# A four-layer audio tower: the third layer's experts, all eight against the two that the gate picks

## The chip, the cores and the metric

One core of one Trainium2 chip runs the whole tower in one launch. The metric is the device time of that launch in microseconds (us), the median of several runs. The five engines (TensorE or PE, VectorE or DVE, ScalarE or ACT, GpSimd or POOL, SyncE or SP) each run a program of their own and meet only at semaphores.

## What is computed

Four sequences of 748 tokens (width 128) pass four layers, each an attention and a feed-forward part. The change is in the third layer's feed-forward part, a mixture of eight experts. Its gate works on the whole sequence: tokens are pooled into one vector for each batch, so that one pair of experts is picked for all 748 tokens. The reference computes all eight experts and multiplies six of them by zero:

```python
def _L2_ffn_ref(x, attn_w, attn_b, gate_w, gate_b, w1, b1, w2, b2):
    scores = x @ attn_w + attn_b
    aw = jax.nn.softmax(scores, axis=1)
    pooled = jnp.sum(x * aw, axis=1)
    gates = jax.nn.softmax(pooled @ gate_w + gate_b, axis=-1)
    _, idx = jax.lax.top_k(gates, 2)
    mask = jnp.sum(jax.nn.one_hot(idx, 8, dtype=gates.dtype), axis=-2)
    g = gates * mask
    g = g / (jnp.sum(g, axis=-1, keepdims=True) + 1e-09)
    h = jax.nn.gelu(jnp.einsum('bsd,edh->ebsh', x, w1) + b1[:, None, None, :], approximate=False)
    eo = jax.nn.gelu(jnp.einsum('ebsh,eho->ebso', h, w2) + b2[:, None, None, :], approximate=False)
    return jnp.einsum('ebso,be->bso', eo, g)
```

The hidden width is 512 (four tiles of 128, `FT`). The fourth layer's experts, whose gate picks for each token, are all computed, before and after.

## The kernel before

All is f32 in this part. The kernel has a front (layers one and two's attention), a long middle (layer two's experts), and from about 2975 us a tail with layers three and four. The tail's work is a list, `TAIL`, that every engine walks in the same order, each doing its own share of a step. It is made of four parts for each batch: part 0 is layer three's attention, with the pooling and the gate at its end (steps `pool` and `gate`); part 1 is layer three's experts (steps `up2`, `down2`, then `back2`, which turns their sum back and adds it to `h`) and a norm (`measure`, `normalise`, `turn`); part 2 is layer four's attention; part 3 is layer four's norm, gate and experts. Part 0 and part 1 of batch 0 stand alone. After that part 2 of batch b - 1 is woven with part 0 of batch b, and part 3 of batch b - 1 with part 1 of batch b. The last batch's parts 2 and 3 stand alone again.

`woven` (line 469) merges two parts by the share of their cost that is done: each step has a cost written by hand in `tail_steps` (line 432), and steps are sorted by the middle of their share. So the order depends on the costs and on the number of steps; nothing is moved while it runs. Even batches use lane 0's buffers, odd ones lane 1's (`k` is the lane).

An expert is four `up2` steps (two matmuls each: 128x128 weights against 384 or 364 columns) and two `down2` steps (four matmuls each, summed in PSUM). ScalarE takes each product out with a gelu, into `hid` or into `outs2`, which are two tiles of `masked`. VectorE's `merge2` (line 2607) copies the expert's gate value into a column, multiplies the expert's output by it and adds it to `sum2` (in `KT`), then frees the weights. TensorE's side of this is `second` (line 1560) with `job`, whose matmul is line 1556; it waits for the result of three matmul groups before, four PSUM banks being in use. The weights of an expert are 128 rows of 1029 values, 514.5 KB. SyncE loads them (`load_second`, line 774) into two slots in turn, as soon as `wts_free` says that a slot is free, so that the first two of a batch are there long before the batch's gate.

`gating_parts` (line 2210) is the gate on VectorE, a chain of tiny steps with a drain behind each: maximum, first pick, then, after ScalarE's exponential, second pick and the gate values. It serves three gates: layer two's, layer three's (one row) and layer four's (six tiles).

`fuse` multiplies pairs of layer four's attention weights together, ahead of their use in part 2. It is made in two portions: `EARLY` (four heads) inside the last norm of batch 0's part 0, `LATE` (four heads) inside the norm at the end of batch 0's part 1. After `LATE` TensorE signals `third_free`, upon which SyncE may load the fourth layer's expert weights (2060 KB) over the third layer's.

SyncE's own program, in order: weights of batch 0's experts; fourth layer's weights after `third_free`; then for b = 1 to 3 the next batch's `hn`, the experts' weights of batch b, and the stores of batch b - 1, which wait for its result.

## Time and profile before

| | before |
|---|---|
| median of 3 runs | 4555.29 us (4553.76 to 4556.07) |
| span of the profiled execution | 4551.8 us |
| PE busy | 4137.7 us, 91% |
| ACT busy | 2872.1 us, 63% |
| DVE busy | 2766.0 us, 61% |
| POOL busy | 708.1 us, 16% |
| DMA moved | 160.46 MB, mean 35 GB/s |
| tail (from 2975 us), by share of the chain that ended last from 3060 us on | PE L1556 28.3% |

The profile is of one execution. Its span runs from the first to the last instruction and is 3.5 us below the median of the runs. Busy times of an engine are sums of durations; TensorE's matmuls overlap one another, so their durations add up to more than the time they take, and their distance from start to start is the better price. An f32 matmul shows as two records. PEclk is the share of the full clock that was granted: 1.00 is 2.4 GHz and 0.50 is 1.2 GHz.

### The profile page before, as it was taken

What the parts mean: (1) busy time and instruction counts of PE and PEld (TensorE: products, weight loads), DVE (VectorE), ACT (ScalarE), POOL (GpSimd) and SP (SyncE); (2) the same over time, 40 slices, a digit from 0 to 9 for tenths busy, and PEclk for the clock granted to TensorE, in tenths of its full rate; (3) what the DMA queues carried; (4) which work ended last, traced back from release to release, by engine and by line L of the source; (5) the groups of instructions that cost most, each with busy time, mean ns of one, the idle gap of its engine ahead of it and who ended that gap; (6) DMA issues with size and microseconds to landing.
All of it is one profiled execution on the core that took longest, in us unless ns stands there. A gap on an engine that the chain in (4) does not pass through costs nothing.

```text
span 4551.8 us, 67714 instructions
## 1 busy us (share of the span) xinstructions
PE 4137.7 (91%) x25107; PEld 2324.2 (51%) x25107; DVE 2766.0 (61%) x6426; ACT 2872.1 (63%) x6118; POOL 708.1 (16%) x484
## 2 busy tenths in 40 slices
PE   7787599999999999999999999868889888988988
PEld 5464344444444444444444444435556555655666
DVE  5656477777777777777777777422442444344254
ACT  3232278777877787777878787674664574474533
POOL 1000212232322222222222232100000000000000
PEclk9878699999999999999999999989999999999999
DMA  2000233333424242424243333000000000000000
GB/s 109 7 21 1 43 45 47 46 52 45 60 43 61 37 60 43 60 39 54 43 53 56 48 50 41 24 32 28 32 1 24 22 1 15 27 1 1 29 4 4
DMA packets 94713, 160.46 MB, mean 35 GB/s; under 512 B 18305, under 2 KB 75058, under 8 KB 94130
## 3 DMA queue, kind: packets, MB, share of 16 engines
q1 hardware_dynamic: 94386, 156.14, 20.6%
q8 instruction: 201, 3.29, 0.3%
q14 instruction: 126, 1.03, 0.1%
HBM read 73.97 MB, written 7.82 MB: 18 GB/s over the span
## 4 chain that ended last, share of the span: by engine, by line
PE 74%; DVE 9%; issue 6%; ACT 6%; DVEq 2%; PEld 1%; POOL 1%; PEldq 0%; DMA 0%; POOLq 0%; SPq 0%; ACTq 0%
PE ps L1190 12%; PE ps L1226 12%; PE ps L1200 10%; PE ps L1556 9%; PE ps L1260 4%; PE ps L1269 4%; PE ps L1181 2%; PE ps L1077 2%; PE ps L1688 2%; PE ps L1488 2%; PE ps L1289 2%; PE ps L1626 1%; DVE peaks L2274 1%; PE ps L1650 1%; PE ps L1062 1%
## 5 line engine op out<-in xcount | busy, mean ns | idle before, releaser
L2274 DVE TENSOR_REDUCE peaks<-ps 128x1 f32<-128x748 f32 (+1 forms) x1536 | 1408.8, 933 | 482.4 <-PE ps L1200 459.5
L1845 ACT ACTIVATE masked<-ps 128x384 f32<-128x384 f32 (+3 forms) x1536 | 683.7, 486 | 193.6 <-PE ps L1190 181.1
L1845 ACT ACTIVATE probs<-ps 128x384 f32<-128x384 f32 (+1 forms) x1536 | 662.4, 484 | 73.9 <-PE ps L1190 73.7
L923 POOL TENSOR_TENSOR rstd<-var,minus_half 128x6 f32<-128x6 f32 x104 | 138.4, 1331 | 2823.8 <-DVE var L2500 1495.0
L1190 PE MATMUL ps<-shared 98*128 98x384 bf16 (+3 forms) x1536 | 447.6, 327 | 4.5 <-ACT probs L1845 1.7
L1190 PE MATMUL ps<-q_stack,k_stack 98*128 98x384 bf16 (+3 forms) x1536 | 450.3, 328 | 1.2
L1200 PE MATMUL ps<-k_stack,q_stack 96*128 96x374 bf16 (+1 forms) x1536 | 380.6, 329 | 35.3 <-DMA k_stack<-parts 21.8
L1200 PE MATMUL ps<-shared 96*128 96x374 bf16 (+1 forms) x1536 | 372.1, 323 | 7.4 <-DVE peaks L2274 6.9
L1190 PEld LDWEIGHTS ps<-shared 98*128 98x128 bf16 (+1 forms) x1536 | 148.0, 103 | 337.2 <-ACT masked L1845 126.2
L1190 PEld LDWEIGHTS ps<-q_stack,k_stack 98*128 98x128 bf16 (+1 forms) x1536 | 149.6, 103 | 329.9 <-ACT masked L1845 121.2
L1200 PEld LDWEIGHTS ps<-k_stack,q_stack 96*128 96x128 bf16 (+1 forms) x1536 | 154.8, 105 | 157.6 <-DVE peaks L2274 42.2
L1200 PEld LDWEIGHTS ps<-shared 96*128 96x128 bf16 (+1 forms) x1536 | 155.9, 104 | 115.5 <-issue 38.1
L1260 PE MATMUL ps<-attT,wr 128*128 128x364 f32 (+1 forms) x512 | 208.8, 492 | 2.7
L1973 ACT ACTIVATE hid<-ps,wts 128x384 f32<-128x384 f32 (+1 forms) x256 | 146.3, 573 | 88.9 <-PE ps L1556 77.6
L1269 PE MATMUL ps<-hid,wr 128*128 128x364 f32 (+1 forms) x512 | 171.0, 477 | 0.0
L1556 PE MATMUL ps<-hid,wts 128*128 128x364 f32 (+1 forms) x512 | 169.9, 479 | 0.0
L1886 ACT ACTIVATE hid<-ps,wr 128x384 f32<-128x384 f32 (+1 forms) x256 | 139.9, 572 | 44.4 <-PE ps L1260 41.1
L1226 PE MATMUL ps<-masked,shared 128*32 128x384 f32 (+3 forms) x1536 | 160.5, 490 | 0.6 <-ACT masked L1845 0.6
L1226 PE MATMUL ps<-masked,V 128*32 128x384 f32 (+3 forms) x1536 | 160.5, 490 | 0.0
L1226 PE MATMUL ps<-probs,V 128*32 128x384 f32 (+1 forms) x1536 | 160.5, 490 | 0.0
L1226 PE MATMUL ps<-probs,shared 128*32 128x384 f32 (+1 forms) x1536 | 160.5, 490 | 0.0
L1556 PEld LDWEIGHTS ps<-hid,wts 128*128 128x128 f32 x512 | 96.7, 192 | 60.5 <-issue 2.3
(584 smaller groups left out, 7646.7 us busy)
## 6 DMA issues: line engine op xcount, KB each, us to landing
shared<-parts SPq DMA_DIRECT2D x192, 187.0 KB, 9.1
wr<-in_l SPq DMA_DIRECT2D x32, 580.5 KB, 3.5
q_stack<-parts SPq DMA_DIRECT2D x96, 187.0 KB, 8.0
k_stack<-parts SPq DMA_DIRECT2D x96, 187.0 KB, 10.5
wts<-in_l SPq DMA_DIRECT2D x32, 514.5 KB, 3.6
wrow<-in_l_rows SPq DMA_DIRECT2D x32, 320.0 KB, 4.0
wq<-in_l SPq DMA_DIRECT2D x32, 192.0 KB, 3.4
shared<-in_tv SPq DMA_DIRECT2D x1, 4096.0 KB, 27.1
```

The costliest lines, as they stand in the source:

```text
L923: pool.tensor_tensor(lane.rstd, lane.var, minus_half[:, :], ALU.pow).then_inc(S["rstd_ready"], 1)
L1077: mm = pe.matmul(ps[:, 4 + t % 4, 0:width], lhs, rhs, start=(i == 0), stop=(i == len(terms) - 1))
L1190: pe.matmul(out[0:m, 0:hi - lo], k_stack[k][0:STACK + SHIFT, head, j * P:j * P + m], q_stack[k][0:STACK + SHIFT, head, lo:hi], start=True, ...
L1200: mm = pe.matmul(out[0:m, a, 0:T // 2], q_stack[k][0:STACK, head, j * P:j * P + m], k_stack[k][0:STACK, head, a * T // 2:(a + 1) * T // 2] ...
L1226: mm = pe.matmul(ps[at:at + PLACE, 6, 0:hi - lo], V32[x % 2][0:m, j, head, :], probs_ring(SIDE * b + i)[0:m, 0:hi - lo], start=(j == 0), s ...
L1260: pe.matmul(out[:, 0:hi - lo], wr[:, WR_UP + f * P:WR_UP + (f + 1) * P], attT[:, lo:hi], start=True, stop=True).then_inc(S["ring_ready"], 1)
L1269: mm = pe.matmul(out[:, 0:hi - lo], wr[:, WR_DOWN + f * P:WR_DOWN + (f + 1) * P], hid[:, f, lo:hi], start=(f == 0), stop=(f == FT - 1))
L1556: mm = pe.matmul(ps[:, bank, 0:hi - lo], w, rhs[:, lo:hi], start=(c == 0), stop=(c == len(terms) - 1))
L1845: act.activation(probs_ring(u)[0:m, 0:hi - lo], src[0:m, 0:hi - lo], ACT.Exp, scale=float(HD) ** -0.5).then_inc(S["ring_done"], 1)
L1886: act.activation(dst[:, lo:hi], src[:, 0:hi - lo], ACT.Gelu, bias=wr[:, bias:bias + 1])\
L1973: act.activation(dst, src, func, **more).then_inc(S[f"feat_done_{k}"], 1)
L2274: v.tensor_reduce(peaks[0:m, g, j, head:head + 1], src[0:m, :, 0:T // 2], XY, ALU.max)\
```

## The change

Only the two experts picked for a batch are computed. VectorE turns each pick's rank (8 for expert 0 down to 1 for expert 7) into the expert's number, an integer in SBUF, and signals `picked_0` or `picked_1` (by lane). SyncE waits for it, reads each number into a register, and loads the weights from the address that follows from it, the first pick into slot 0, the second into slot 1. The gate values of the two picks are reduced to a column each, which `merge2` uses in place of the copied one. In the list, batch 0's part 1 now begins with the late fusing, which leaves the norm at its end; part 1 of the other batches begins with a step `picked` on which no engine does anything, but which has a cost of 5.0 for `woven`. With two experts in place of eight, part 1's cost falls from 95.3 to 36.7, and `woven` lays it out against part 3 in another order.

```diff
+TOP = 2
...
     if part == 1:
-        steps = []
-        for e in range(E):
+
+        steps = [(("fuse", LATE), 12.0)] if b == 0 else [(("picked",), 5.0)]
+        for e in range(TOP):
             steps += [(("up2", e, i), 1.35) for i in range(FT)] + [(("down2", e, i), 2.6) for i in range(2)]
         steps.append((("back2",), 3.0))
-        return steps + norm_steps("h", *([(("fuse", LATE), 12.0)] if b == 0 else []))
+        return steps + norm_steps("h")
...
+        picks = sb("picks", [P, LANES, TOP], mybir.dt.int32)
+        pick_gates = sb("pick_gates", [P, LANES, TOP])
...
-            def load_second(e):
-
-                sp.wait_ge(S["wts_free"], n.take("wts_free"))
-                sp.dma_start(wts[:, e % 2, 0:W2_END], A["l2"][e, :, :]).then_inc(S[f"wts_loaded{e % 2}"], 16)
+            def load_second(b):
+
+                k = b % 2
+                sp.wait_ge(S[f"picked_{k}"], n.take(f"picked_{k}"))
+                for i in range(TOP):
+                    e = sp.value_load(tails[k].picks[0:1, i:i + 1], min_val=0, max_val=E - 1)
+                    sp.wait_ge(S["wts_free"], n.take("wts_free"))
+                    sp.dma_start(wts[:, i, 0:W2_END], A["l2"][bass.ds(e, 1), :, :].rearrange("o p n -> (o p) n"))\
+                        .then_inc(S[f"wts_loaded{i}"], 16)
...
-            for e in range(E):
-                load_second(e)
+            load_second(0)
...
-                for e in range(E):
-                    load_second(e)
+                load_second(b)
                 store(b - 1)
...
-                        n.take(f"feat_done_{k}", 2 * (FT + 1) * E)
+                        n.take(f"feat_done_{k}", 2 * (FT + 1) * TOP)
...
                 first_of_largest(L, PK)
+                if picks is not None:
+                    step(v.tensor_scalar(picks[:, 0:1], M, -1.0, float(E), ALU.mult, ALU.add))
                 yield
...
                 step(v.tensor_reduce(M, CD, X, ALU.max))
+                if picks is not None:
+                    step(v.tensor_scalar(picks[:, 1:2], M, -1.0, float(E), ALU.mult, ALU.add))
+                    v.drain().then_inc(S["picked" + of], 1)
...
                 over_sum(gates[:, :, 0:tiles].rearrange("p e t -> p t e"), EX, EX, 1e-9 if over_all else 0.0)
+                if picks is not None:
+
+                    own = gates[:, :, 0:tiles].rearrange("p e t -> p t e")
+                    step(v.tensor_tensor(PK, PK, CD, ALU.subtract))
+                    for i, one in enumerate((PK, CD)):
+                        step(v.tensor_tensor(L2, own, one, ALU.mult))
+                        step(v.tensor_reduce(pick_gates[:, i:i + 1], L2, X, ALU.add))
                 yield
...
                 def merge2(lane, k, e):
 
-                    column(lane, e, 1)
                     v.wait_ge(S[f"feat_done_{k}"], n.take(f"feat_done_{k}", 2 * (FT + 1)))
+                    gate = lane.pick_gates[:, e:e + 1]
                     if e == 0:
-                        v.tensor_scalar(sum2[:, 0:T], outs2[0][:, 0:T], lane.gcol[:, 0:1], None, ALU.mult)
+                        v.tensor_scalar(sum2[:, 0:T], outs2[0][:, 0:T], gate, None, ALU.mult)
...
                 def back2(lane, k):
-                    merge2(lane, k, E - 1)
+                    merge2(lane, k, TOP - 1)
```

The order of one woven stretch (part 3 of batch 0, A, with part 1 of batch 1, B) begins, before: B up2 (0,0), B up2 (0,1), A measure, B up2 (0,2), (0,3), B down2 (0,0), A normalise, B down2 (0,1), B up2 (1,0), A turn, and so on. After: A measure, B picked, A normalise, A turn, B up2 (0,0), A logits, A up4 (0,0), B up2 (0,1), A gate, A up4 (0,1), A gate, B up2 (0,2), ... It ends, before: B back2, A up4 (7,1), down4 (6,1), B measure, A down4 (7,0), B normalise, A down4 (7,1), B turn. After: B back2, A up4 (6,0), down4 (5,0), up4 (6,1), B measure, A down4 (5,1), up4 (7,0), down4 (6,0), up4 (7,1), B normalise, A down4 (6,1), (7,0), (7,1), B turn.

## Rows read from the trace of the kernel before

**Rows 1.** Stages by time: length, busy us of PE, PEld, DVE, ACT, POOL, PEclk, DMA.

```profile
3102.00:3186.00 84.00, 82.92 (x256) 49.56 (x256) 11.98 (x39) 47.77 (x83) 0.00 (x0) 0.97 0.13 38
3434.00:3567.00 133.00, 130.41 (x540) 87.18 (x540) 31.49 (x107) 69.05 (x120) 1.32 (x1) 0.97 0.09 25
3815.00:3949.00 134.00, 131.41 (x532) 87.68 (x531) 31.58 (x107) 68.56 (x119) 1.32 (x1) 0.96 0.08 24
4497.00:4552.00 55.00, 48.96 (x285) 38.27 (x284) 20.50 (x78) 19.42 (x35) 0.00 (x0) 0.93 0.03 8
```

**Rows 2.** Groups by line of the stretch 3434 to 3567: busy, mean | idle before, releaser.

```profile
L1556 PE MATMUL ps<-k_stack,wts 128*128 128x364 f32 (+1 forms) x128 | 46.1, 502 | 0.0
L1556 PE MATMUL ps<-hid,wts 128*128 128x364 f32 (+1 forms) x128 | 42.5, 478 | 0.0
L1973 ACT ACTIVATE hid<-ps,wts 128x384 f32<-128x384 f32 (+1 forms) x64 | 36.6, 573 | 28.0 <-PE ps L1556 25.4
...
L1667 PE MATMUL ps<-const,xnT 128*128 128x8 f32 x12 | 2.3, 266 | 0.0
L1666 PE MATMUL ps<-rows,const 1*128 1x8 f32 x12 | 2.3, 262 | 0.0
```

**Rows 3.** The chain of work, longest pieces: start, us, what, records.

```profile
3101.95 82.98 PE ps L1556 x256
...
3471.35 5.03 PE ps L1556 x16
```

**Rows 4.** Timeline at batch 0's gate: start, us, engine, line [idle before <-releaser].

```profile
3101.95 7.57 PE L1556 MATMUL ps<-xnT,wts 128*128 128x384 f32 x16 [0.30 <-issue]
...
3105.53 0.16 DVE L2249 TENSOR_REDUCE m<-cand 128x1 f32<-128x8 f32 x1
3105.77 0.17 DVE L2250 TENSOR_TENSOR cand<-cand,m 128x8 f32<-128x8 f32 x1
```

**Rows 5.** The weights' tile: its loads' issue ns, and us to landing.

```profile
L777 SPq DMA_DIRECT2D wts<-in_l x32: 327/328/650, 2977.6 to 4298.9; - x32
...
DMA to landing us min/median/max: 3.4/3.6/10.9
```

**Rows 6.** Timeline, late heads fused beside batch 0's norm.

```profile
3187.44 0.82 PE L1145 MATMUL ps<-const,shared 128*128 128x128 f32 x6
...
3191.29 0.39 PE L1150 MATMUL ps<-shared,q_stack 128*128 128x128 f32 x2
...
3193.68 0.88 PE L1445 MATMUL ps<-const,xn 128*128 128x128 f32 x6 [2.00 <-DVEq L2491]
```

**Rows 7.** Timeline at the start of the first woven stretch.

```profile
3429.64 0.16 DVE L2249 TENSOR_REDUCE wrow<-wrow 128x1 f32<-128x8 f32 x1
...
3432.71 1.62 PE L1626 MATMUL ps<-x,shared 128*128 128x128 f32 x6 [4.11 <-DVE shared L2633]
...
3434.12 6.97 PE L1556 MATMUL ps<-k_stack,wts 128*128 128x384 f32 x16
...
3438.69 1.63 DVE L2505 TENSOR_SCALAR xn<-h,mv,rstd 128x128 f32<-128x128 f32 x6 [1.44 <-POOL rstd L923]
```

**Rows 8.** Stretches by time again, for the granted clock (PEclk) alone.

```profile
3434.00:3436.00 2.00, 2.00 (x5) 1.13 (x5) 1.19 (x6) 0.36 (x1) 0.00 (x0) 0.50 0.01 4
4494.00:4499.00 5.00, 5.00 (x20) 4.76 (x21) 0.00 (x0) 0.00 (x0) 0.00 (x0) 0.50 0.02 3
```

**Rows 9.** Timeline at the start of the last stretch.

```profile
4490.88 1.54 PE L1445 MATMUL ps<-const,k_stack 128*128 128x128 f32 x6 [5.71 <-DVEq L2491]
...
4493.08 0.56 PE L1666 MATMUL ps<-rows,const 1*128 1x8 f32 x2 [0.66 <-ACT k_stack L1977]
...
4499.25 6.04 PE L1556 MATMUL ps<-k_stack,shared 128*128 128x384 f32 x12
```

**Rows 10.** Timeline at the end of the first woven stretch.

```profile
3574.04 1.41 PE L1445 MATMUL ps<-const,k_stack 128*128 128x128 f32 x6 [3.55 <-DVEq L2491]
...
3576.06 2.83 PE L1639 MATMUL ps<-k_stack,shared 128*128 128x384 f32 x4 [0.61 <-ACT k_stack L1977]
```

More of the change, by code:

```diff
@@ L518 @@
     gcol: object
+    picks: object
+    pick_gates: object
 def cut(ap, n):
@@ L704, in lane_small @@
             return dict(stats=stats_s[:, k, :, :], mv=mv_s[:, k, :, :], var=var_s[:, k, :], rstd=rstd_s[:, k, :],
-                        half_sum=half_sums[:, k, :], pooled=pooled_s[:, k, :], **small(k))
+                        half_sum=half_sums[:, k, :], pooled=pooled_s[:, k, :], picks=picks[:, k, :],
+                        pick_gates=pick_gates[:, k, :], **small(k))
         tails = (
@@ L2208, in attention, with gating_parts @@
                 v.drain()
-            def gating_parts(tiles, over_all, lg, lg2, ex, pick, cand, m1, gates, of=""):
+            def gating_parts(tiles, over_all, lg, lg2, ex, pick, cand, m1, gates, of="", picks=None, pick_gates=None):
                 logits_ready, exps_ready = "logits_ready" + of, "exps_ready" + of
@@ L2603, in gate @@
                     if i == 0:
-                        gating[k] = gating_parts(1 if part == 0 else NT, part == 0, *lane.gating, lane.gates, f"_{k}")
+                        chosen = (lane.picks, lane.pick_gates) if part == 0 else ()
+                        gating[k] = gating_parts(1 if part == 0 else NT, part == 0, *lane.gating, lane.gates, f"_{k}",
+                                                 *chosen)
                     next(gating[k])
                 def merge2(lane, k, e):
-                    column(lane, e, 1)
                     v.wait_ge(S[f"feat_done_{k}"], n.take(f"feat_done_{k}", 2 * (FT + 1)))
+                    gate = lane.pick_gates[:, e:e + 1]
                     if e == 0:
-                        v.tensor_scalar(sum2[:, 0:T], outs2[0][:, 0:T], lane.gcol[:, 0:1], None, ALU.mult)
+                        v.tensor_scalar(sum2[:, 0:T], outs2[0][:, 0:T], gate, None, ALU.mult)
                     else:
-                        v.scalar_tensor_tensor(sum2[:, 0:T], outs2[e % 2][:, 0:T], lane.gcol[:, 0:1], sum2[:, 0:T],
+                        v.scalar_tensor_tensor(sum2[:, 0:T], outs2[e % 2][:, 0:T], gate, sum2[:, 0:T],
                                                ALU.mult, ALU.add)
```

2 lines of the change are left out of this document (1 added, 1 removed).

## The prediction, made before the changed kernel ran

> **What bounds the kernel now.** I read the stage table first [rows 1]. The third layer's experts run in four stretches: batch 0's alone (3102 to 3186 us), and those of batches 1, 2 and 3, each woven with the fourth layer of the batch before (about 133 us each). In all four TensorE is busy nearly throughout (82.9 of 84, 130.4 of 133, 131.4 of 134, the last like it), while ScalarE is busy half the time and VectorE a quarter. So here a matmul that goes away should take its own time with it. The groups of one such stretch say the same: ScalarE's gelus into `hid` waited 25.4 us for TensorE, and the expert matmuls hardly waited [rows 2].
>
> **What is removed.** An f32 matmul of 384 or 364 columns shows as two records; an expert has 16, so 32 records (128 plus 128 in a stretch, for eight experts [rows 2]). Busy sums overlap, so I price by the chain of work, where one stands behind the other: 16 records take 5.03 us, 0.315 us each [rows 3]. An expert is 32 x 0.315 = 10.1 us, six are 60.4 us. Batch 0's eight experts took 82.98 us [rows 3], which is 80.6 and a slow start. Six experts' gelus on ScalarE (10 of 0.573 us each [rows 2]), merges on VectorE and 24 of 32 weight fetches go too, off the path. Four batches: 241.6 us leave TensorE.
>
> **What is added, batch 0.** Before, the experts start at 3101.95, while the gate is still being computed; their weights had been loaded long before. Now they wait for the picks. The second pick's maximum ends at 3105.69 (3105.53 + 0.16), and a step of this VectorE chain takes 0.24 us, start to start [rows 4]. One added step lies ahead of it and one makes the second pick: the pick semaphore comes at about 3106.3. Then SyncE reads a register from SBUF and issues the load, and the load lands 3.6 us after issue (3.4 at least; the 10.9 is one that stood behind others) [rows 5]. Nothing in the trace shows SyncE reading SBUF. The nearest rows are its own issue (0.33 us) and a whole memory round trip with data (3.4 us) [rows 5]; I bound waking, reading and forming the address by 0.3 and 3.4 us, and take 1.4, nearer the short end because one word moves. Not below nothing: no such read is done now. The first weights stand at 3106.3 + 1.4 + 3.6 = 3111.3, so 9.4 us of delay (8.3 to 11.4). The second expert's load comes 1 to 3 us later and is needed 10 us later. Fusing the late heads, which is moved ahead of the experts, lies inside that delay: its matmuls run from 3187.44 to 3191.68 now [rows 6], 4.2 us, perhaps 7 at the lower clock. It costs nothing where it leaves, either: it ran beside a norm that is late by itself (TensorE still sat idle 2.00 us behind it for VectorE [rows 6]). Its four ScalarE copies per pair of heads stand ahead of the first gelu, in the same wait. Batch 0 gives 60.4 - 9.4 = 51.0 us.
>
> The Trainium skill ("Runtime: NRT & Kernel Launch", section "Instruction fetch mechanics") gives about 200 ns for one register load from HBM; no row here shows one. By it the 1.4 us would be some 0.6, an estimate, and the whole sum 0.8 us better.
>
> **What is added, batches 1 to 3.** Here the order changes as well. Now eight small pieces of expert work hide the other batch's norm at the start; with a quarter of the work the weave puts measure, normalise and turn of that norm first, and the experts' first matmuls behind them.
> - Idle start: the last attention matmuls end at about 3434.3 and today the experts follow at once. The norm runs beside them: measured, POOL's power, and normalised from 3438.69 for 1.63 us [rows 7]. After, TensorE waits for it until about 3440.4: +6.1 us.
> - The picks are hidden here. The pick's maximum ends near 3429.8 [rows 7]; plus 0.5, 1.4 and 3.6 is 3435.3, five us before the norm is through. SyncE has nothing else queued: the stores of batch b - 1 stand behind the fetch in its program, those of b - 2 are over. That slack also covers a slower read.
> - Clock: at this start the granted clock is 0.50, which is 1.2 GHz [rows 8]; the 16 records take 6.97 us [rows 7] where 16 warm ones take 5.03. The nearest row of the new order (idle, norm, turn, logits, then wide matmuls) is the last stretch: 5.71 us idle, turn 1.54 us against 0.88 [rows 6], clock 0.50 through the logits [rows 8], which take 6.2 us (4493.08 to 4499.25) against 2.3 + 2.3 in a woven stretch [rows 2, 9], then 12 records in 6.04 against 3.8 [rows 9]. That is 4.6, and 0.6 for the expert piece ahead of the logits: 5.2, of which 1.9 is paid already: +3.3 us, between nothing and 5.
> - The gate's added steps stand on the path (TensorE sat 4.11 us idle for VectorE at just that place [rows 7]): two for the picks, five for the two gate values, 7 x 0.24 = +1.7 us.
> - In the middle ScalarE's exponential with its two table loads has fewer gelus around it: +1.0 us, from 0 to 3, taken by hand from the order.
> - The end gets better. Now TensorE sits idle 3.55 us for the expert batch's norm, and the next stretch then starts slowly [rows 10]. In the new order ten fourth-layer pieces of about 1.3 us follow the transposes of the experts' sum, and the norm's chain of some 6 us lies under them: -3.5, -0.5 for faster transposes, and -2.3 for the next stretch's first matmuls (2.83 us for four records against 1.3 warm, and those behind). The wait ahead of those transposes stays, for in both orders two merges come before them.
>
> Each gives 60.4 - 6.1 - 3.3 - 1.7 - 1.0 + 6.3 = 54.6 us, three 163.8. What is left of the stretch, 79 us, holds 71 of matmuls, and ScalarE falls to 35, so no other engine becomes the bound. Loads of the fourth layer's weights are issued earlier, behind batch 0's two fetches, into room that is free once the heads are fused.
>
> **The sum.** 51.0 + 163.8 = 214.8 us off the profiled span of 4551.8; the median of the runs, 4555.3, lies 3.5 above it, and I keep that. 4555.3 - 214.8 = 4340.5.
>
> **The rivals.**
> 1. Slow fetch: the read and a load by a register's address take 10 us more than I say. Batch 0 pays all, the others what is beyond their 5 us of slack: 10 + 3 x 5 = 25, so 4365. For it: no such load is in the trace. Against: the loads' rows and sizes stay the same, 514.5 KB.
> 2. Low clock: TensorE, let idle for the weights, stays at 1.2 GHz through most of the first expert instead of its first 16 records. At half speed an expert costs 10.1 us more, of which 2 to 3 are in my sum: 4 x 7 = 28, so 4368. For: in the last stretch the level was 0.50 through turn and logits [rows 8], some 8 us. Against: batch 0's first 16 records took 7.57 us, so the engine was back at full speed within them [rows 4]. The Trainium skill ("TensorE: Matmul & The Clock Gate", section "Loop structure matters more than you think") speaks against this change: a wait on a DMA ahead of matmuls lets the clock drop and they run cold. The trace agrees as to the start, and bears out a price of 2 to 3 us.
> 3. The gaps fill better: clock and middle cost nothing new, and the fetch is at its short end: 3 x 4.3 + 1 = 14 less, so 4326.
> 4. Other side: the fetch alone eats the gain. The place is SyncE between pick and landing, in each batch; batch 0 pays F, the others F - 5. It decides from F + 3(F - 5) = 215, F = 57 us above my 5. At F = 65 the time is 4585. It takes a load that goes in far smaller pieces because its address is in a register; against it, the access pattern has the same 128 rows.
> 5. It doesn't do what it says, that is the stretches keep their length because the fourth layer's own chain sets them. Alone (last stretch) that layer had TensorE busy 49.0 of 55 us [rows 1], so at most its bubbles come back, 6 us a stretch: 4358. A computation that stays whole is excluded, since the loops over experts are unrolled.
>
> **How the numbers follow.** Forecast with its own bounds (4328 to 4355) 0.58; slow fetch 0.09; low clock 0.09; better filling 0.14; bubbles 0.08; slower 0.02. The predicted time is 4340. The range takes the filling case (4326, with a margin of 8 for a matmul price that is 1% off and three starts), and reaches up to the slow cases at 4368: 4318 to 4370. Only rival 4 isn't faster by over 0.2% (9 us, about what a measurement of this kernel can tell from no change): faster 0.98, same 0.005, slower 0.015.
>
> **What would show it.** Right: 192 x 4 fewer expert records; batch 0's experts start 9 to 10 us after the gate's matmul and take 21 us; woven stretches of about 79 us with TensorE idle 6 us at the start for the norm, not for a DMA, and no idle time at the turn of the end; 8 weight loads landing in 3.6 us. Wrong: an idle time at a woven start that ends with the weights (fetch over 10 us), stretches over 88 us with TensorE waiting for ScalarE or VectorE, or the attention stretches changing by more than 3 us.

## The result and the profile after

The changed kernel took 4327.25 us (median of four runs, 4326.6 to 4328.9) against 4554.97: a ratio of 0.9499, 95% interval 0.9486 to 0.9513. That is 227.7 us less, where the forecast was 214.8 less, 4340. The profiled span is 4325.5 us, 1.75 us below the median, where before it was 3.5. Each run here lies 2.0 us above its own span, so the difference between 1.75 and 3.5 is which execution was profiled: before it was the fastest (4553.76 us against a span of 4551.8).

To see where the time went I cut both spans at the same instructions and took the windows between them. The cuts: batch 0's gate matmul (before at 3101.05, after at 3100.56); "back", the transposes of batch 0's expert sum; q0 to q3, a batch's first query matmul of the fourth layer's attention; w0 to w3, the last weighing matmuls of that attention; and the end. From w to the next q is a woven stretch, from q to w an attention stretch, in which the change removes nothing.

| stretch | before, us | after, us | gained | forecast |
|---|---|---|---|---|
| start to gate | 3101.05 | 3100.56 | 0.5 | 0 |
| gate to back (batch 0's experts) | 85.68 | 34.95 | 50.7 | 51.0 |
| back to q0 | 8.43 | 9.10 | -0.7 | 0 |
| q0 to w0, attention | 237.55 | 239.53 | -2.0 | -1.7 |
| w0 to q1, woven | 143.35 | 87.06 | 56.3 | 54.0 |
| q1 to w1, attention | 237.38 | 234.38 | 3.0 | 0.6 |
| w1 to q2, woven | 145.90 | 89.75 | 56.2 | 54.0 |
| q2 to w2, attention | 236.72 | 233.92 | 2.8 | 0.6 |
| w2 to q3, woven | 145.71 | 87.07 | 58.6 | 54.0 |
| q3 to w3, attention | 142.49 | 139.83 | 2.7 | 2.3 |
| w3 to end | 67.49 | 69.40 | -1.9 | 0 |

The forecast column is the prediction's 51.0 and three times 54.6, laid out by these cuts: the gate's added steps (-1.7) fall ahead of w, the next stretch's first matmuls (+2.3) behind q.

Of the page, the line of engines. TensorE is still the bound, 90% busy; it has 768 records fewer than before (24339 against 25107), the 4 x 192 of the six experts.

```profile
PE 3887.6 (90%) x24339; PEld 2172.9 (50%) x24339; DVE 2742.4 (63%) x6398; ACT 2735.0 (63%) x5878; POOL 707.8 (16%) x484
```

Stages by time: length, busy us of PE, PEld, DVE, ACT, POOL, then PEclk, DMA share, GB/s. The first row is batch 0's experts, then come the three woven stretches and the attention stretch between the first two:

```profile
3100.00:3136.00 36.00, 30.04 (x98) 19.66 (x99) 7.08 (x35) 17.82 (x32) 0.00 (x0) 0.82 0.29 99
...
3384.10:3471.20 87.10, 76.59 (x388) 56.43 (x388) 31.36 (x124) 36.61 (x62) 2.64 (x2) 0.91 0.02 6
3471.20:3705.60 234.40, 195.12 (x1353) 133.65 (x1353) 113.44 (x366) 141.34 (x263) 2.64 (x2) 0.96 0.02 7
3705.60:3795.30 89.70, 79.49 (x387) 58.21 (x387) 31.45 (x123) 36.61 (x62) 2.64 (x2) 0.88 0.02 6
4029.30:4116.30 87.00, 76.54 (x387) 56.37 (x387) 31.36 (x123) 36.60 (x62) 2.64 (x2) 0.91 0.02 6
```

The same cuts in the kernel before, for the woven stretches (longer than the windows of [rows 1], since they reach from cut to cut):

```profile
3432.70:3576.10 143.40, 136.65 (x580) 92.85 (x580) 38.66 (x139) 69.60 (x121) 2.64 (x2) 0.96 0.08 23
...
3813.40:3959.30 145.90, 139.14 (x579) 94.64 (x579) 38.82 (x141) 69.60 (x121) 2.64 (x2) 0.94 0.08 22
4196.10:4341.80 145.70, 138.94 (x580) 94.54 (x580) 38.40 (x137) 69.59 (x121) 2.64 (x2) 0.95 0.08 22
```

Length minus PE busy is TensorE's idle time: 6.8 us in each of before, 10.5, 10.2 and 10.5 after. ScalarE has half its old work in a stretch (36.6 for 69.6 us) and is no bound. TensorE's mean granted clock is lower than before (0.91, 0.88, 0.91 for 0.96, 0.94, 0.95).

**Batch 0.** Timeline at its gate (start, us, engine, line, [idle before <-releaser]), to compare with [rows 4]:

```profile
3105.27 0.16 DVE L2261 TENSOR_REDUCE m<-cand 128x1 f32<-128x8 f32 x1
3105.50 0.15 DVE L2263 TENSOR_SCALAR picks<-m 128x1 int32<-128x1 f32 x1
3106.78 1.50 SPq L788 DMA_DIRECT2D wts<-in_l  x2
3110.65 7.97 PE L1566 MATMUL ps<-xnT,wts 128*128 128x384 f32 x16 [3.42 <-DMA wts<-in_l]
3135.51 0.88 PE L1596 MATMUL ps<-const,KT 128*128 128x128 f32 x6 [1.81 <-DVEq L2513]
```

The second pick is there at 3105.65, SyncE's first issue starts 1.1 us later, and the experts start at 3110.65, 10.09 us behind the gate's matmul (3100.56). Before it was 0.90 (3101.95 against 3101.05). The delay is 9.2 us; 9.4 was forecast. The first 16 records take 7.97 us, where they took 7.57 before [rows 4].

**The weights' tile,** against [rows 5]: 8 loads where there were 32, issue 338 to 376 ns, landing 3.5 to 5.2 us.

```profile
L788 SPq MOVE wts<-in_l x8: 29/29/46, 3106.7 to 4027.1; - x8
L788 SPq DMA_DIRECT2D wts<-in_l x8: 338/351/376, 3106.8 to 4027.2; - x8
...
DMA to landing us min/median/max: 3.5/4.0/5.2
```

**Start of the first woven stretch,** against [rows 7]:

```profile
3380.77 1.45 SPq L788 DMA_DIRECT2D wts<-in_l  x2
3384.14 1.62 PE L1636 MATMUL ps<-x,shared 128*128 128x128 f32 x6 [5.62 <-DVE shared L2657]
...
3391.48 1.54 PE L1455 MATMUL ps<-const,xn 128*128 128x128 f32 x6 [5.71 <-DVEq L2513]
3392.81 2.76 PE L1566 MATMUL ps<-k_stack,wts 128*128 128x384 f32 x4
...
3399.45 2.91 PE L1566 MATMUL ps<-xnT,shared 128*128 128x384 f32 x4
```

The weights were asked for at 3380.77, and the first load landed 3.5 us later, at 3384.3, 8.5 us ahead of its first use at 3392.81. What TensorE waits for is VectorE: 5.62 us in front of the last weighing matmuls (before 4.11 [rows 7]) and 5.71 us for the fourth layer's normalise. The turn and the first expert piece then run at the low clock (1.54 us, and 2.76 for four records), as in the last stretch [rows 9].

**End of the first woven stretch,** against [rows 10]. First the two lines of before that followed those of [rows 10], then after:

```profile
3579.84 2.93 PE L1643 MATMUL ps<-shared,k_stack 128*128 128x128 f32 x12 [0.94 <-ACT q_stack L2066]
3583.67 1.61 PE L1650 MATMUL ps<-k_stack,q_stack 128*128 128x374 f32 x2 [0.90 <-ACT q_stack L2068]
```

```profile
3469.42 0.82 PE L1455 MATMUL ps<-const,k_stack 128*128 128x128 f32 x6
3471.20 1.52 PE L1649 MATMUL ps<-k_stack,shared 128*128 128x384 f32 x4 [0.95 <-DVE k_stack L2533]
3473.66 1.60 PE L1653 MATMUL ps<-shared,k_stack 128*128 128x128 f32 x12 [0.94 <-ACT q_stack L2076]
3476.17 1.53 PE L1660 MATMUL ps<-k_stack,q_stack 128*128 128x374 f32 x4 [0.90 <-ACT q_stack L2078]
```

The idle 3.55 us ahead of the transposes (line 1445 before, 1455 after) are gone, and the next stretch starts at full speed: the first two groups take 1.52 and 1.60 us where they took 2.83 [rows 10] and 2.93, the third 1.53 for four records where two took 1.61.

### The profile page after: what moved, and what is told of

It reads as the page before. It is cut to its first block, busy times and chain, and to the rows that moved or that the text cites. A ratio compares the mean times of both kernels' runs of the same rounds, so it can differ in the third digit from the quotient of the medians.

```text
span 4325.5 us, 65880 instructions
## 1 busy us (share of the span) xinstructions
PE 3887.6 (90%) x24339; PEld 2172.9 (50%) x24339; DVE 2742.4 (63%) x6398; ACT 2735.0 (63%) x5878; POOL 707.8 (16%) x484
## 4 chain that ended last, share of the span: by engine, by line
PE 72%; DVE 10%; issue 6%; ACT 6%; DVEq 2%; PEld 1%; POOL 1%; DMA 0%; PEldq 0%; POOLq 0%; SPq 0%; ACTq 0%
PE ps L1200 13%; PE ps L1236 13%; PE ps L1210 11%; PE ps L1270 4%; PE ps L1566 4%; PE ps L1279 4%; PE ps L1191 3%; PE ps L1087 2%; PE ps L1698 2%; PE ps L1299 2%; PE ps L1498 2%; DVE peaks L2296 2%; PE ps L1636 2%; PE ps L1660 2%; PE ps L1072 1%
## 5 line engine op out<-in xcount | busy, mean ns | idle before, releaser
L1896 ACT ACTIVATE KT<-ps,wr 128x384 f32<-128x384 f32 x64 | 36.7, 573 | 143.7 <-PE ps L1279 143.7
L1279 PEld LDWEIGHTS ps<-hid,wr 128*128 128x128 f32 x512 | 95.4, 190 | 51.8
L1299 PE MATMUL ps<-xnT,wq 128*128 128x384 f32 (+1 forms) x256 | 106.4, 502 | 16.3 <-issue 15.6
## 6 DMA issues: line engine op xcount, KB each, us to landing
k_stack<-parts SPq DMA_DIRECT2D x96, 187.0 KB, 10.5
wts<-in_l SPq DMA_DIRECT2D x8, 514.5 KB, 4.0
```

Of the source, the lines that this page charges most:

```text
L1279: mm = pe.matmul(out[:, 0:hi - lo], wr[:, WR_DOWN + f * P:WR_DOWN + (f + 1) * P], hid[:, f, lo:hi], start=(f == 0), stop=(f == FT - 1))
L1299: pe.matmul(out[:, 0:hi - lo], w, xT_[:, lo:hi], start=True, stop=True).then_inc(S["ring_ready"], 1)
L1896: act.activation(dst[:, lo:hi], src[:, 0:hi - lo], ACT.Gelu, bias=wr[:, bias:bias + 1])\
```

## Experiments

The theory: a removed matmul is worth its spacing in the chain (0.315 us a record); the fetch delays the experts by about 9 us once, in batch 0, and is hidden elsewhere; and what the woven stretches lose is order (the norm in front of the experts) and the clock behind idle time. The rivals: the fetch costs in every stretch, or the last margin is something else than the change. Diffs are against the changed kernel unless said otherwise; times are medians, ratios are to the kernel before, intervals are 95%. In the profiles of these kernels batch 0's gate matmul, ahead of which nothing but nudge touches the work, lies between 3098.1 and 3106.3 us, so I judge by the stretches and not by the total where a few us matter. A stretch is read from one execution, and the four executions of one kernel can lie 9 to 16 us apart (nudge, fixed, six_reads); where the profiled one is not near the median, I say so.

**only_two: the removal alone.** The kernel before, without the picks: experts 0 and 1 in each batch, whatever the gate says.

```diff
+TOP = 2
-        for e in range(E):
+        for e in range(TOP):
```
(and the four other places that count experts)

> The kernel before with one part alone: experts 0 and 1 of the third layer are computed for every batch, the other six and their fetches are left out (so the output is another one). No pick, no fetch that waits for it, no added gate steps, the late heads fused at the end as before, and the weave without the step for the picks. If the removed matmuls are worth their own time, the four stretches lose 60.4 us each, batch 0 pays no 9.2 us for its weights and the woven stretches begin with expert pieces beside the other batch's norm: 26 us under the changed kernel, about 4301 (4294 to 4308). Rival, the fourth layer's chain is the bound of the woven stretches once the cover is thin: no faster than the changed kernel there, so about 4318.

It took 4291.1 us (4288.0 to 4291.8), ratio 0.9424 [0.9409, 0.9440].

```profile
3102.00:3127.30 25.30, 23.17 (x67) 13.68 (x67) 5.86 (x28) 14.14 (x23) 0.00 (x0) 0.89 0.00 0
...
3374.00:3453.10 79.10, 74.71 (x387) 55.23 (x388) 31.54 (x126) 35.72 (x61) 2.64 (x2) 0.96 0.00 1
```

Gate to back went from 85.68 to 25.28: 60.4 us for six experts, the price of the prediction to the tenth. The woven stretches (79.2, 79.2, 79.2) fell by 64 to 67, more than 60.4: TensorE's idle time in them fell from 6.8 to 4.4 us, since the wait for the norm at the end is gone, and its busy time by 62 to 64.5, less of it being at the low clock. What the changed kernel has above 4291, 36 us, comes with the rest of the change, that is the picks, their fetch, the gate's steps, the moved fusing and the step in the weave: 9.7 in batch 0, and 7.9, 10.6 and 7.9 in the woven stretches. I had set this kernel 10 us too high.

**fixed: no pick, no register.** The same order of work, but SyncE fetches experts 0 and 1 by constant addresses, and waits for no pick.

```diff
-                sp.wait_ge(S[f"picked_{k}"], n.take(f"picked_{k}"))
-                    e = sp.value_load(tails[k].picks[0:1, i:i + 1], min_val=0, max_val=E - 1)
-                    sp.dma_start(wts[:, i, 0:W2_END], A["l2"][bass.ds(e, 1), :, :].rearrange("o p n -> (o p) n"))\
+                    sp.dma_start(wts[:, i, 0:W2_END], A["l2"][i, :, :])\
```

> The changed kernel, but SyncE fetches experts 0 and 1 by a constant address as soon as the slots are free, and waits for no pick and reads no register (so the output is another one); the gate's added steps stay. Dependency theory: batch 0's experts start when the late heads are fused, 3.4 us earlier, and the woven stretches don't change, for the weights were there before the norm was through: 4323.9 (4322 to 4326). Rival, the register reads or the picked fetches disturb the woven stretches too: more than 6 us faster.

It took 4319.0 (4316.7 to 4330.6), ratio 0.9496 [0.9477, 0.9515]; the profile is of its fastest execution. That interval overlaps the changed kernel's, so the total alone tells nothing here. Gate to back is 29.55 instead of 34.95, so batch 0 pays 5.4 us for the fetch, half of it idle time and half a busy time that a lower clock draws out (26.9 against 29.6). The first and third woven stretch stay: 87.08 and 86.99 against 87.06 and 87.07. The fetch is hidden there. The second is 86.8 instead of 89.75 and the first attention stretch 234.7 instead of 239.5, but not for a wait that went: the second's idle time is 10.5 us against 10.2, and TensorE's busy time fell by 3.2. (six_reads has 234.8 for that attention stretch too, with a longer fetch.) What is left over only_two's 25.28, 4.3 us, is the fusing of the late heads, which now stands in front of the experts: with the weights long there, they still start 7.4 us behind the gate.

**six_reads: the read made six times as dear.**

```diff
-                    e = sp.value_load(tails[k].picks[0:1, i:i + 1], min_val=0, max_val=E - 1)
+                    for _ in range(6):
+                        e = sp.value_load(tails[k].picks[0:1, i:i + 1], min_val=0, max_val=E - 1)
```

> The changed kernel with each pick read six times by SyncE ahead of its load. It gives the price r of one read: the first load of a batch is issued 5 r later. Only batch 0 waits for its weights (3.4 us of idle time there); the woven stretches have some 7 us between landing and first use. With r near 0.7 us batch 0 pays 3.5 and the others nothing: 4331. Rival 1 of the prediction (a slow fetch), r of 2 us: batch 0 pays 10, the others 3 each, 4346.

It took 4333.1 (4324.0 to 4339.8; the profiled execution 4329.5). The register reads are records of their own in the line's list (ns: least, median, most):

```profile
L787 SPq TENSOR_LOAD <-picks x48: 261/266/485, 3111.5 to 4034.5; - x48
```

From the gate's matmul to the first issue it is now 9.0 us (3106.3 to 3115.32) instead of 6.2 (3100.56 to 3106.78): 2.8 for five more reads, so one read is 0.56 us in all, of which the load itself is 0.27. Batch 0 was idle 6.0 us for the weights instead of 3.4, though gate to back grew by 1.4 us only (36.3 for 34.96), because TensorE's busy time in it fell by 1.2. The woven stretches didn't move (87.1, 89.8, 87.0): 5.5 us more reading for the two picks, and still nothing there waited for it. The Trainium skill ("Runtime: NRT & Kernel Launch", section "Instruction fetch mechanics") gives about 200 ns for a register load from HBM; these, from SBUF, take 266, and the whole read twice that.

It also shows what the address in a register does to a load. The changed kernel issues the two loads of a pair 1.1 us apart, six_reads 3.9 us apart, and fixed, by constant addresses, some 0.5 us apart in three of its four pairs. Time to landing, fixed and then six_reads, against the 3.5/4.0/5.2 above:

```profile
DMA to landing us min/median/max: 3.5/4.5/9.6
```

```profile
DMA to landing us min/median/max: 3.5/3.5/3.6
```

So a load by a register's address lands in the same 3.5 us when it is alone. What takes 4.4 to 5.2 us in the changed kernel is the second of each pair, which runs beside the first; the second constant load of fixed's close pairs took 4.4 to 5.6 us, and 9.6 beside other loads.

**no_cost: the place holder taken out of the weave.** The changed kernel's weave begins batches 1 to 3 with a step `("picked",)` that issues nothing on TensorE and counts as 5.0 us, time set aside for the picks and the fetch. Without it:

```diff
-        steps = [(("fuse", LATE), 12.0)] if b == 0 else [(("picked",), 5.0)]
+        steps = [(("fuse", LATE), 12.0)] if b == 0 else []
```

> The changed kernel with the step for the picks taken out of the weave, so that three expert pieces of 1.3 us stand among measure, normalise and turn of the other batch's norm at the start of a woven stretch. Nothing else changes. If TensorE's 5.7 us there are idle only because of the order, 3.9 us come back in each of three stretches: 4315.5 (4312 to 4320). Rival, the weights (issue about 4.8 us ahead of the end of the attention, landing in 3.5 to 5.2) come too late and TensorE waits for them in place of the norm: half of it or nothing, 4321 to 4328.

It took 4298.5 (4297.7 to 4303.8), ratio 0.9446 [0.9430, 0.9462]: 28.8 us less than the changed kernel, and 17 less than I expected.

```profile
3382.10:3462.50 80.40, 77.20 (x388) 57.03 (x388) 31.24 (x124) 35.72 (x61) 2.64 (x2) 0.93 0.02 6
3696.70:3774.30 77.60, 74.03 (x388) 54.84 (x388) 31.26 (x124) 35.60 (x61) 2.64 (x2) 0.97 0.02 7
4009.10:4088.40 79.30, 76.24 (x388) 56.26 (x388) 31.18 (x123) 35.61 (x61) 2.64 (x2) 0.94 0.02 7
```

Idle time is 3.2, 3.6 and 3.1 us where it was 10.5, 10.2 and 10.5, which makes 21 of the 28.8 us; 5 more are clock, nearly all of it in the second stretch (74.0 us busy for 79.5). The timeline says why the idle time went:

```profile
3378.69 1.45 SPq L788 DMA_DIRECT2D wts<-in_l  x2
...
3382.07 1.62 PE L1636 MATMUL ps<-x,shared 128*128 128x128 f32 x6 [5.62 <-DVE shared L2657]
3383.48 5.78 PE L1566 MATMUL ps<-k_stack,wts 128*128 128x384 f32 x12
3389.40 0.88 PE L1455 MATMUL ps<-const,xn 128*128 128x128 f32 x6
```

The experts follow the attention at once, without waiting for weights, and the norm is ready when they are done. The cover is thin now: the first load, issued at 3378.69, landed 3.5 us later, at 3382.2, and was used at 3383.48, 1.3 us on. What I had put down to the smaller expert work (the norm first, +6.1) was this one step of the weave.

**gates_later: five VectorE steps moved behind the first merge.** The gate values aren't needed before the first expert's sum.

```diff
@@ gate, between the gate values of all experts and the five steps
+                yield
@@ merge of the experts
+                    if e == 0:
+                        next(gating[k])
```

> The changed kernel with the five VectorE steps that form the two gate values moved from the gate to the first merge of the experts, where VectorE waits anyway. If these steps stand on the path at the end of the attention stretches (idle of TensorE there 5.6 us against 4.1 before), 5 x 0.24 us come back three times: 3.6 less, 4323.6, and that idle time falls to 4.4. Rival, the path there is TensorE's own and VectorE's steps are beside it: no change of the idle time, 4327.

It took 4334.1 (4330.2 to 4336.2), slower by 7, not faster by 4. The wait ahead of the last weighing matmuls did fall, 5.6 to 4.4 us. But the woven stretches are 90.6, 88.0 and 90.6 instead of 87.1, 89.75 and 87.1. The first of them, to stand beside the changed kernel's above:

```profile
3385.30:3475.90 90.60, 79.86 (x387) 59.17 (x387) 32.33 (x128) 36.57 (x62) 2.64 (x2) 0.87 0.03 10
```

TensorE is busy 79.9 us instead of 76.6 with as many records. The window of the logits, first here, then in the changed kernel:

```profile
3397.00:3403.00 6.00, 6.00 (x24) 5.72 (x24) 0.00 (x0) 0.58 (x1) 0.00 (x0) 0.50 0.00 0
```

```profile
3395.50:3399.40 3.90, 3.90 (x25) 3.66 (x24) 0.00 (x0) 0.58 (x1) 0.00 (x0) 0.94 0.00 0
```

The same logits, in the same order, behind nearly the same idle time (6.04 and 5.71 us): at 0.50, which is 1.2 GHz, here and at 0.94 there. 2.1 of the 3.3 us arise there. This is the start that the prediction priced at +3.3 us. The changed kernel has it in no stretch: the first and third take 87.1 us, and the second, 89.75, is slow only behind its logits.

**warm_start: work in the idle time.** Four dummy matmuls of 384 columns, into a bank nobody reads, ahead of the turn.

```diff
+                        if part == 3 and b < B - 1:
+                            for _ in range(4):
+                                pe.matmul(ps[:, 1, 0:384], ident, C("tok_w")[:, 0:384], start=True, stop=True)
```

> The changed kernel with four f32 matmuls of 384 columns into an unused PSUM bank ahead of the turn that waits for the norm at the start of each woven stretch, about 5 us of work at the low clock in 5.7 us of idle time. If the fallen clock costs there what turn and first expert piece show (1.33 for 0.67 and 2.7 for 1.3 us), 2 us come back three times: 4321. If the idle time alone counts and the clock is nothing, 4327; if the fillers run past the norm they cost up to 1 each, 4330.

It took 4319.5 (4313.8 to 4322.0). The turn and the first expert piece are then at full speed (0.87 and 1.46 us, where it was 1.54 and 2.76):

```profile
3382.94 4.46 PE L1737 MATMUL ps<-const 128*128 128x384 f32 x8
...
3388.87 0.87 PE L1455 MATMUL ps<-const,xn 128*128 128x128 f32 x6 [1.46 <-DVEq L2516]
3389.58 1.46 PE L1566 MATMUL ps<-k_stack,wts 128*128 128x384 f32 x4
```

The stretches are 86.4, 83.2, 86.4. So the dummies bring 0.7 us in the stretches that were at speed behind the start anyway, and 6.5 in the second, which was not; its clock is 0.97 now, where it was 0.88. The profile is of the fastest execution, 5.7 us below the median, so 7.8 us of the total is the safer figure.

**norm_last: idle time put back at the end.** In the woven stretches the experts' normalise is moved to just in front of its turn.

```diff
@@ woven, for each pair with an expert part
+        out.remove((b, 1, ("normalise", "h")))
+        out.insert(out.index((b, 1, ("turn",))), (b, 1, ("normalise", "h")))
```

> The changed kernel with one VectorE step moved: the normalise of the experts' norm stands right ahead of its turn, behind the fourth layer's last merges, in the three woven stretches. TensorE then sits idle about 2.9 us ahead of that turn. If the idle time lets the clock fall as it did before the change, each stretch pays 2.9, 0.5 for slower transposes and 4.0 in the next attention's first matmuls: +22, 4349. Without a fall of the clock: +9, 4336.

It took 4352.1 (4351.1 to 4355.2), ratio 0.9562 [0.9546, 0.9578]: 25 more, near the first of the two values.

```profile
3469.93 0.88 PE L1460 MATMUL ps<-const,k_stack 128*128 128x128 f32 x6 [2.71 <-DVEq L2518]
3471.41 2.11 PE L1654 MATMUL ps<-k_stack,shared 128*128 128x384 f32 x4 [0.61 <-DVE k_stack L2538]
3474.47 2.93 PE L1658 MATMUL ps<-shared,k_stack 128*128 128x128 f32 x12 [0.94 <-ACT q_stack L2081]
3478.30 2.86 PE L1665 MATMUL ps<-k_stack,q_stack 128*128 128x374 f32 x4 [0.90 <-ACT q_stack L2083]
```

2.71 us of idle time, and the three groups behind it take 7.90 us instead of the changed kernel's 4.65, much as in the kernel before. The woven stretch is 2.6 us longer, and the attention stretch that begins with them is 240.5 us long instead of 234.4: 6 us more again. The other two woven stretches are 93.6 and 93.5 instead of 89.75 and 87.1. The Trainium skill ("TensorE: Matmul & The Clock Gate", section "Loop structure matters more than you think") says that matmuls with a long wait for a DMA between them run cold. Here the wait is for a norm and 2.71 us long, and the rows agree.

**fuse_late: the heads fused in their old place.** `("fuse", LATE)` of batch 0 goes back behind the norm.

```diff
-        steps = [(("fuse", LATE), 12.0)] if b == 0 else [(("picked",), 5.0)]
+        steps = [] if b == 0 else [(("picked",), 5.0)]
-        return steps + norm_steps("h")
+        return steps + norm_steps("h", *([(("fuse", LATE), 12.0)] if b == 0 else []))
```

> The changed kernel with the late heads fused inside the norm at the end of batch 0's experts, as before the change. If either place is cover (a wait for weights of 9 us at the start, a norm of 6 us at the end), the time stays within 2 us of the changed kernel's: 4327, with TensorE idle 9 us ahead of batch 0's experts. Rival, moving it gained its own matmul time: 4.2 us more or up to 7, 4331 to 4334.

It took 4335.0 (4331.9 to 4337.4).

```profile
3110.27 2.26 PE L1566 MATMUL ps<-xnT,wts 128*128 128x384 f32 x3 [9.34 <-DMA wts<-in_l]
```

TensorE now waits 9.34 us for the weights, idle instead of fusing, and gate to back stays at 34.97. Back to q0 falls from 9.10 to 8.44, the value of before. So the moved fusing costs 0.7 us where it left and nothing where it went. The total rose all the same, by 7.8, and in stretches that this edit doesn't touch: 90.3, 90.3 and 87.0 woven, 237.4 in the attention behind the first.

**again and nudge: does the place in time matter?** After gates_later and fuse_late I asked whether such a rise comes with a run or with a kernel. again is the changed kernel once more. nudge puts five tiny VectorE writes (1.2 us) ahead of batch 0's pooling and changes nothing else.

```diff
+                        if b == 0 and at[0] == 0:
+                            for _ in range(5):
+                                v.memset(lane.pooled[:, 3:4], 0.0)
+                                v.drain()
```

> The changed kernel itself, once more and on the chip of the three kernels beside it. Every theory: 4327, within 3 us, since its four runs lay between 4326.6 and 4328.9. If the kernel's woven stretches come out at 87 in one run and at 90 in the next, it lies up to 10 us higher.

> The changed kernel with five tiny VectorE steps ahead of batch 0's pooling, which shift all that follows by 1.2 us and alter nothing else. If the length of TensorE's slow stretches depends on the order of the work alone, 1.2 us more: 4328.5. If it depends on where in time they fall, the woven stretches change between about 87 and 90.5 us though their order is the same, and the total moves by 3 to 10 us in either direction.

again took 4327.2 (4324.2 to 4329.0), with woven stretches of 87.0, 89.75 and 87.0 again. nudge took 4331.7 (4329.3 to 4338.2), and in the profile its woven stretches were 89.0, 90.3 and 87.0, its attention stretches 237.2 and 235.2 against 234.4 and 233.9:

```profile
3388.80:3477.80 89.00, 78.03 (x388) 57.53 (x388) 31.37 (x123) 36.66 (x62) 2.64 (x2) 0.90 0.01 4
3477.80:3715.00 237.20, 198.76 (x1353) 136.15 (x1353) 113.56 (x366) 141.68 (x263) 2.65 (x2) 0.94 0.02 7
```

So the order within a stretch doesn't fix its length: the order is the same here, and the same work comes out 3 us apart, at granted clocks of 0.94 and 0.96. In two profiles the changed kernel had the same lengths, and its eight executions lie within 5 us. But nudge's profile is of its slowest execution, 6.5 us above the median, and its four spread over 9 us. Its runs all lie above those eight, by 0.3 us at least, so the total did move; how much of what its profile shows comes from the touch, and how much from that one execution, is not shown.

**both: no_cost and gates_later together.**

> The two edits of the runs before together: no step for the picks in the weave, and the gate values formed in the first merge. If they act at different places they add up: 4298.5 less 3.6, 4295 (4291 to 4298). If the shorter gate only lets the weights' wait show (they land as the attention ends), it stays at 4298.

It took 4295.8 (4295.5 to 4297.3), ratio 0.9431 [0.9416, 0.9447], the best version that still chooses: 31.5 us under the changed kernel. All its runs lie below no_cost's, but by little: the medians are 2.7 us apart, where no_cost's own runs spread over 6. It is 4.7 us above only_two, which chooses nothing. The cover of the fetch is used up in it: in each woven stretch the experts start 0.13 us behind the landing of their first load, as in batch 0, and 1.5 to 1.7 us behind the start of the last weighing matmuls where no_cost has 1.4.

**split_logits: the narrow matmuls spread out.** On top of both, the logits in three portions with pieces of wide matmuls in between.

```diff
-    steps = norm_steps("h") + [(("logits",), 1.2)]
+    steps = norm_steps("h") + [(("logits", 0), 0.4), (("up4", 0, 0), 1.35), (("logits", 1), 0.4),
+                               (("up4", 0, 1), 1.35), (("logits", 2), 0.4)]
```
(and the logits step itself, in portions of two tiles)

> The version without the pick step and with the late gate values (4295.8), in which the 24 narrow matmuls of the fourth layer's gate stand in three portions with fourth-layer pieces of 384 columns between them, in all four of its stretches. If the stretch of narrow matmuls (3.8 us, or 6.3 at the low clock) is what lets the clock fall behind them, each of four stretches gets back 1 to 3 us: 4288 (4284 to 4292). If the fall comes from the idle time ahead of them, nothing changes: 4296.

It took 4304.4 (4303.1 to 4307.7), 8.6 more than both. Where I had aimed it works: the woven stretches are 78.5, 79.8 and 78.5 where both has 79.5, 80.6 and 81.0. The last part, where the logits are split too, takes 71.9 instead of 69.4, and more is lost in attention stretches whose order is the same: 238.3, 234.5 and 235.4 for 235.1, 231.7 and 229.5. The third of them, in both and then in split_logits:

```profile
3773.80:4003.30 229.50, 192.02 (x1353) 131.05 (x1353) 112.56 (x361) 142.51 (x264) 2.64 (x2) 0.98 0.01 3
```

```profile
3776.80:4012.20 235.40, 197.90 (x1353) 135.69 (x1353) 112.62 (x361) 142.63 (x264) 2.64 (x2) 0.95 0.01 3
```

Idle time is 37.5 us in each; the 5.9 us are TensorE's busy time, and the granted clock is 0.98 against 0.95.

## Why the prediction was right

The mechanism held and the size was 13 us short (4327 against 4340, 6% of the gain). The time is that of rival 3, "the gaps fill better" (4326), but only its cheap clock came true: the idle time was as forecast. Point by point:

- **A removed matmul is worth its spacing: right.** 0.315 us a record from the chain [rows 3] gives 60.4 us for six experts; only_two measured 60.4 in batch 0. (The busy figures of the views count overlapping time once and are not sums of durations: 128 records of 502 ns in the mean show as 46.1 us [rows 2]. Groups overlap one another all the same, so the spacing was the right price.)
- **Batch 0: right, 50.7 against 51.0.** The 1.4 us between pick and issue were 1.1; the landing was 3.7, not 3.6. Fetch and fusing hide each other: without the fetch 5.4 us come back (fixed), without the fusing none (fuse_late, 34.97). "It costs nothing where it leaves" was 0.7 us out (back to q0).
- **The fetch is hidden in the woven stretches: right.** fixed takes it away, six_reads adds 5.5 us to it; the first and third stay at 87.0 to 87.1 in both. Rivals 1 and 4 fall with that, and rival 2 with batch 0's first 16 records, 7.97 us where a lasting low clock was to draw out the whole expert. Rival 5 does as well: the idle time of a woven stretch grew by 3.7 us, which the sum had, and not by 6 more.
- **The gate's added steps: right.** Idle time ahead of the last weighing matmuls rose from 4.11 to 5.62, 1.5 against 1.7.
- **Idle time of a woven stretch: right in size, wrong in its reason.** Forecast +6.1 at the start, +1.0 in the middle and -3.5 at the end, 3.6; measured 10.5 less 6.8, 3.7. But I laid the +6.1 to the smaller expert work. no_cost shows that the step of 5.0 in the weave makes it: without it the idle time is 3.1 to 3.6, below that of before.
- **Clock of the woven stretches: mis-sized.** I added 3.3 us and took off 0.5 for faster transposes. TensorE's busy time less the expert matmuls' 60.4 was 76.2, 78.7 and 78.5 before; after it is 76.6, 79.5 and 76.5. That is +0.4, +0.8 and -2.0 where I had +2.8. In all 9 of the 13 us, the largest error. The working was off too: I priced the 24 logits at full clock by 2.3 + 2.3 us of busy time, but start to start they take 3.7 (3383.33 to 3387.05 in only_two), so such a start costs 0.9 us more than I wrote. With the right price the forecast would have been 2.7 us farther off. The loss of 3.3 exists (gates_later, 90.6 against 87.1), but whether a stretch has it isn't fixed by its order, and the kernel before paid such a loss in its second and third stretches too, as 139 busy against 136.7 shows. I took the last stretch [rows 8, 9] as the pattern for all three. In the changed kernel it held for none of them: the logits ran at full clock in the first and third stretch and nearly to their end in the second.
- **The next stretch's first matmuls: mis-sized.** I gave 2.3 back, 1.5 of it for the first group. Three groups went from 2.83, 2.93 and about 2.9 (norm_last has 2.86 for the third) to 1.52, 1.60 and 1.53: 4.0. Less 1.5 for the gate's steps and with 0.3 to 0.5 of clock the two attention stretches behind them gained 3.0 and 2.8, not 0.6 each: 4.6 us.
- **The offset between span and runs** was 1.75, not 3.5: another 1.7 us, which is not the kernel's. A run lies 2.0 us above its own span, and I had kept the 3.5 of a profile taken on the fastest execution.
- **Against it** went the first attention stretch (-0.3), back to q0 (-0.7) and the last part (-1.9), all by a few tenths of clock or idle.

Of the signs I had named, the records, the start of batch 0's experts, the idle time for the norm and the end without idle time came as written. Batch 0's experts took 23.1 us, not 21, since their slow start stays, and the loads landed in 4.0 us in the median, not 3.6. ("About 79 us" is by the windows of [rows 1], some 10 us shorter than these cuts.) The attention stretches, of which I had allowed 3 us, changed by just that; I had taken their clock as fixed. The runs here have them between 229.5 and 240.5 us with the same matmuls in the same order.

**Where the cold phases lie.** In each woven stretch the low level begins in the waits at the end of the attention. In the changed kernel's first stretch it ends where the logits begin, and comes back once behind them (the 2.91 us for four records at 3399.45); in gates_later it runs on through them, 27 us in one piece. The changed kernel first:

```profile
3379.00:3396.00 17.00, 6.14 (x18) 4.18 (x18) 8.15 (x42) 2.73 (x4) 1.32 (x1) 0.50 0.19 62
3396.00:3399.40 3.40, 3.40 (x23) 3.17 (x23) 0.00 (x0) 0.20 (x1) 0.00 (x0) 1.00 0.00 0
```

```profile
3381.40:3408.60 27.20, 17.24 (x49) 12.61 (x50) 9.09 (x44) 4.66 (x7) 1.32 (x1) 0.50 0.11 39
```

The second fall doesn't come from idle time. In no_cost's first stretch TensorE was busy 6.66 of 6.80 us ahead of it, the last 2.5 of them with the 8-column logits, and all the time behind it:

```profile
3387.10:3393.90 6.80, 6.66 (x33) 4.57 (x31) 2.18 (x7) 3.89 (x7) 0.55 (x1) 1.00 0.00 1
3393.90:3400.70 6.80, 6.80 (x18) 4.58 (x18) 1.64 (x8) 2.35 (x3) 0.00 (x0) 0.50 0.00 0
```

With the logits in three portions, the first and third stretch of split_logits had no second fall at all.

**What stays open.** Whether a woven stretch gets one long cold phase or two short ones. The order alone does not decide it (nudge); idle time ahead of a group does in part (norm_last, warm_start), and so do the narrow matmuls (no_cost, split_logits), yet the version that spread them lost elsewhere what it won. The changed kernel's pattern came back in a second profile (again), but chance from run to run is not excluded for the others, whose executions lie up to 16 us apart. No run here can tell the remaining causes apart.

## What to carry to other kernels

Where TensorE is busy nearly throughout, price a removed matmul by its spacing in the chain: in batch 0, where it was busy 99% of the time, that was right to a per cent, and in the woven stretches the removal alone gave 4 to 6 us more. Then ask which gaps the new order opens, and what they do to the clock. A choice that is fetched through SyncE costs, here, 1.1 us from pick to issue and 3.5 to 3.7 us of landing; look first at whether the weights would be there anyway, before work is reordered or time set aside to hide them, for here the time set aside cost 29 us and the fetch 5. And judge an edit of a few us by the stretch it touches, not by the total: in split_logits three attention stretches that the edit didn't touch took 12 us more.

## What the runs showed of the hardware that was not expected

- A register read from SBUF by SyncE is 0.56 us in all, 0.27 of it the load (six_reads); a load of 514.5 KB by a register's address lands in 3.5 us, as constant ones do, when it is alone (six_reads), and the second of two issued 1.1 us apart in 4.4 to 5.2 us.
- An idle TensorE of 2.7 us came with 6 us more in the stretch behind it, 3.2 of them in the first three groups (norm_last).
- TensorE's clock fell to 0.50 in the middle of a run of 8-column matmuls, with the engine busy 6.66 of the 6.80 us before (no_cost).
- Identical orders of work ran at different granted clocks. The changed kernel's stretches repeated in a second profile (again: 87.0, 89.75, 87.0) and were others in nudge's (89.0, 90.3, 87.0). Attention stretches of one and the same order were 229.5 to 240.5 us long, at clocks from 0.98 down to 0.92.
